# Reading the tile table two tiles ahead on TensorE, with the values kept in registers

## What is computed

```python
g = jnp.einsum('th,ehf->tef', x, w_gate)
u = jnp.einsum('th,ehf->tef', x, w_up)
act = jax.nn.silu(g) * u
act = act * combine[:, :, None]
moe_out = jnp.einsum('tef,efh->th', act, w_down)
```

## Time and profile before

| what | value |
|---|---|
| median of 3 runs | 1234.64 us (1233.26 to 1236.93) |
| the profiled execution | 1233.21 us, its span 1231.5 us |
| PE busy | 1161.2 us, 94% of the span |
| DVE, POOL, ACT busy | 729.4, 607.4, 512.1 us |
| mean granted TensorE clock | 0.994 of full speed |
| one product as the records show it | up (L1553) 399 ns, down (L1576) 390 ns, row turn (L1534) 276 ns |
| one result stored (L1035) | 256 KB, 2.1 us from issue to landing |

### The profile page before, as it was taken

The page is one execution under the profiler, slowest core; times in us unless marked ns, Lnnn a source line. Parts: engine busy times, 40 slices in busy tenths (PEclk is TensorE's granted clock), DMA queues, the critical chain, the costliest instruction groups (busy, mean ns, idle before and its releaser), DMA issues.

```text
span 1231.5 us, 21807 instructions
## 1 busy us (share of the span) xinstructions
PE 1161.2 (94%) x6020; PEld 776.9 (63%) x6021; DVE 729.4 (59%) x1083; ACT 512.1 (42%) x1056; POOL 607.4 (49%) x603
## 2 busy tenths in 40 slices
PE   1899999999999979999999999999999999999996
PEld 0334343433433346887888787877878777878885
DVE  5888888888888506773444433333333333338877
ACT  1577777777777731111111133333333333321110
POOL 3245645555454244056757345545644745228653
PEclk9999999999999999999999999999999999999998
DMA  9466676766675109944735155455454464433555
GB/s 236 127 189 184 194 192 187 186 189 193 180 193 164 58 35 361 379 161 132 266 127 188 53 161 205 153 189 185 165 193 154 162 209 157 145 94 106 161 170 188
DMA packets 104815, 214.58 MB, mean 174 GB/s; under 512 B 12352, under 2 KB 17472, under 8 KB 104768
## 3 DMA queue, kind: packets, MB, share of 16 engines
q1 hardware_dynamic: 85408, 152.08, 40.2%
q0 software_dynamic: 18016, 61.88, 15.4%
q10 hardware_dynamic: 1344, 0.04, 0.1%
HBM read 117.48 MB, written 91.75 MB: 170 GB/s over the span
## 4 chain that ended last, share of the span: by engine, by line
PE 61%; DVE 1%; issue 1%; DVEq 0%; ACT 0%
PE score_ps L135 19%; PE score_ps L1553 18%; PE d_ps L1508 9%; PE d_ps L1576 9%; PE score_ps L1534 3%; PE d_ps L1565 1%; PE d_ps L1461 1%; DVE y_all L1355 1%; DVE y_all L1343 0%; DVEq L158 0%; PE d_ps L1484 0%; PE score_ps L1470 0%; PE d_ps L1478 0%; DVE th L1420 0%; PE d_ps L1477 0%
## 5 line engine op out<-in xcount | busy, mean ns | idle before, releaser
L662 DVE TENSOR_REDUCE maxima<-score_ps 128x2 f32<-128x1024 f32 x256 | 301.5, 1218 | 49.8 <-PE score_ps L754 47.0
L609 ACT ACTIVATE probs<-sb_ps 128x512 f32<-128x512 f32 x512 | 262.8, 600 | 27.4 <-PE sb_ps L781 27.4
L135 PE MATMUL score_ps<-yn_t,w_split 128*128 128x512 f32 x1056 | 252.9, 398 | 3.1 <-POOL w_split L539 3.1
L1553 PE MATMUL score_ps<-w_split,x_split 128*128 x948 | 236.8, 399 | 0.0
L135 PEld LDWEIGHTS score_ps<-yn_t,w_split 128*128 128x128 f32 x1056 | 199.1, 189 | 51.6 <-POOL w_split L539 4.0
L1553 PEld LDWEIGHTS score_ps<-w_split,x_split 128*128 128x128 f32 x948 | 172.4, 188 | 33.1
L1072 POOL CAST w_split<-w_raw 128x1024 fp32r<-128x1024 f32 x63 | 65.9, 1046 | 241.8 <-POOLq L1142 141.4
L1074 POOL TENSOR_TENSOR w_split<-w_raw,w_split 128x1024 fp32r<-128x1024 f32 x63 | 151.9, 2410 | 5.2
L792 PE MATMUL o_ps<-probs,v_t 128*17 128x512 f32 x1024 | 135.6, 601 | 0.0
L1508 PE MATMUL d_ps<-w_split,h_split 128*128 128x512 f32 x528 | 124.4, 391 | 0.0
L1576 PE MATMUL d_ps<-w_split,h_rows 128*128 x474 | 120.4, 390 | 0.0
(11 more groups left out here) (149 smaller groups left out, 1324.3 us busy)
## 6 DMA issues: line engine op xcount, KB each, us to landing
xs_dram<-zero SPq DMA_DIRECT2D x1, 20224.0 KB, 58.7
stage<-xs_dram SPq DMA_DIRECT2D x79, 256.0 KB, 2.7
res_dram<-stage SPq DMA_DIRECT2D x79, 256.0 KB, 2.1
k_dram<-k_hi SPq DMA_DIRECT2D x16, 512.0 KB, 2.8
q_dram<-q_hi SPq DMA_DIRECT2D x16, 512.0 KB, 2.8
w_raw<-in_L_ffn_w_gate_dram POOLq DMA_DIRECT2D x16, 512.0 KB, 4.8
w_raw<-in_L_ffn_w_up_dram POOLq DMA_DIRECT2D x16, 512.0 KB, 6.1
w_raw<-in_L_ffn_w_down_dram POOLq DMA_DIRECT2D x16, 512.0 KB, 6.8
```

Source lines behind the costliest of these rows:

```text
L135: mm = pe.matmul(dst[i], w[:, k, f * P:(f + 1) * P], self.yn_t[:, b, k, t * self.SPAN:(t + 1) * self.SPAN], start=(n == 0), stop=(n == 3 * ...
L609: act.activation(probs[:, c % 2, head(j)[2], :], sb_ps[:, bank_of_score(HG * c + j), :], ACT.Exp, scale=SCALE).then_inc(exp_done, 1)
L662: dve.tensor_reduce(maxima[q % 2][:, :].rearrange("p (h u) -> p u h", u=8)[:, u, :], sa_ps[:, pair_of_unit(q, g, u), :, :], AX_X, ALU.max) ...
L1553: mm = pe.matmul(gu_ps[j], x_split[j][:, b, k, :], w_split[:, bass.ds(at + (a * 3 * ex.PIECE + k * 2 * FE), 2 * FE)], start=(n == 0), stop ...
```

## The change

PE reads both numbers of tile i + 2 between the up products of tile i + 1 and the down products of tile i. What was read is handed from tile to tile: `at` of the tile whose down products come next, and `need` and `at` of the tile after it. Over the loop's end three registers (`kept`) hold them. The third reading per tile (L1569) is gone, and none is left between the down products and the row turns.

```diff
+        def kept_values():
+
+            at, then = (pe.snap(kept[n], min_val=0, max_val=BUFFER) for n in (0, 2))
+            return at, (pe.snap(kept[1], min_val=3 * FIRST + 3, max_val=3 * (FIRST + NE)), then)
+
...
-        def down_rows(i, j):
-            at = pe.value_load(tables[0:1, bass.ds(i + P, 1)], min_val=0, max_val=BUFFER)
+        def down_rows(i, j, at):
...
-        def tile(i, j):
+        kept = [pe.alloc_register(f"kept{n}") for n in range(3)]
+        def tile(i, j, at, following):
             last = isinstance(i, int) and i == NTILE - 1
-            following = None if last else weights_of(i + 1)
             if ahead(i):
                 turn_rows(i + 2, j)
             turn_hidden(i, j)
-            if not last:
-                up(i + 1, 1 - j, following)
-                down_rows(i, j)
+            if last:
+                return None, None
+            up(i + 1, 1 - j, following)
+            second = weights_of(i + 2) if ahead(i) else None
+            down_rows(i, j, at)
+            return following[1], second
...
-        up(0, 0, weights_of(0))
+        at = weights_of(0)
+        following = weights_of(1)
+        up(0, 0, at)
+        at = at[1]
         for i in range(2):
-            tile(i, i)
+            at, following = tile(i, i, at, following)
+        for reg, value in zip(kept, (at, *following)):
+            pe.reg_mov(reg, value)
         with pe.Fori(1, (NTILE - 3) // 2) as r:
+            at, following = kept_values()
             for j in range(2):
                 pair[0] = r
-                tile(2 * r + j, j)
+                at, following = tile(2 * r + j, j, at, following)
+            for reg, value in zip(kept, (at, *following)):
+                pe.reg_mov(reg, value)
+        at, following = kept_values()
         for i in range(NTILE - 3, NTILE):
-            tile(i, i % 2)
+            last_at = at
+            at, following = tile(i, i % 2, at, following)
...
-        down_rows(NTILE - 1, (NTILE - 1) % 2)
+        down_rows(NTILE - 1, (NTILE - 1) % 2, last_at)
```

## The result

The changed kernel takes 1238.51 us (median of 8 runs, 1236.74 to 1241.13), the kernel before 1234.97 us (8 runs). The ratio is 1.0031, with a 95% interval of 1.0018 to 1.0044: 3.8 us slower by the ratio. It had 1236.5 us.

What follows compares the result with a forecast made beforehand. PE bounds the kernel, busy 94%, with its sequencer late at even tiles' row turns. Tiles 0, long loads +1.6, second meetings +0.8, less about 0.5, gave +1.9 on 1234.64: 1236.5 us, range 1229 to 1242.

Steps and rivals of the forecast that it cites:

- The loop's end: Late even-tile row turns cost 0.33 us per pair, 12.2 us in all; the hidden-values wait limits PE's gain to 5.2 us.
- The readings' new place: With a second 0.75 us reading between up and down products, the sequencer sets the even tile's down products' start, where it was.
- even tile 0: Term of the sum: the even tile's 0.14 us PE gain is waited away ahead of its down products, net 0.
- came out 0.02 early: Even tile's down products at 822.45 against 822.47 before; about 0.5 us was taken off the sum for it.
- The odd tile: Its two readings have room, since its load takes 302 ns and PE bounds what follows; counted as nothing.
- Slow loads: A reading that meets the store costs 0.27 us more; long even-tile loads over 580 ns add 1.57 us.
- the rival of 1246.5 us: Both readings of the even tile are slow, 0.27 us per pair, 10 us in all; chance 0.13.
- second meetings: Second readings that meet the late store's packets in perhaps one tile in twelve: 3 x 0.27 = 0.8 us.
- The readings fit: Rival: down products wait for PE again and the 5.2 us stay, 1229.4 us; chance 0.25.
- All of the 12.2 us: Rival: the hidden-values wait is earlier than thought, so all the loop's-end loss comes back, 1222.4 us; chance 0.03.
- nothing moves: Rival: the branch, not the even tile's first readings, held the row turns, 1234.6 us; chance 0.04.
- The sum: Even and odd tile 0, long loads +1.6, second meeting +0.8, less about 0.5: about +1.9 us.

Runs made afterwards that it cites:

- split kernel: Changed kernel, but only `at` is read between up and down products and `need` behind the down products: 1229.04 us, ratio 0.9953 to the kernel before.
- kernels with the waits first: Up products' waits for split weights and rows put ahead of the hidden-values wait: 1225.48 us with `need` read behind the down products, 1233.70 us in the changed kernel.
- kernels that split only one kind of tile: Changed kernel with `need` read behind the down products in even tiles only, 1228.88 us, or in odd tiles only, 1240.23 us.
- two kernels with a late store: SP issues the result's store only after the split of the next hidden values: 1248.31 us in the kernel before, 1237.95 us in the changed kernel.
- kernels with a third reading: Changed kernel plus one more, unused reading of `at` per tile between up and down products: 1264.44 us, ratio 1.0233 to the kernel before.
- both readings under the wait: Changed kernel with both readings moved behind the row turns, ahead of the wait for the hidden values: 1233.19 us, ratio 0.9981 to the kernel before.
- both readings behind the down products: Changed kernel with both readings moved from between up and down products to behind the down products: 1241.24 us, ratio 1.0048 to the kernel before.

## Why the prediction was right, and where it was off

**The loop's end.** Right. The 0.33 us ahead of the even tile's turns are gone, and not 12.2 us but about 5 are there to be won from it. The split kernel, where nothing else gets in the way, is 5.8 us faster by the ratio (1 - 0.9953), against 5.2 in the forecast. That the hidden values and the instructions behind their wait hold the up products is shown by the kernels with the waits first. The up products came 0.20 us earlier on the record, not 0.14, but as the forecast said this was waited away ahead of the down products.

**The readings' new place.** Right in mechanism, and mis-sized in one term. The forecast let the sequencer release the even tile's down products at the time of before, which makes a pair of 9.92 us plus the long loads. Measured over the loop it is 10.04, and the median of the single pairs has gone from 9.90 to 10.00. The term "even tile 0" is the one that was off: it measured 0.1 us per pair, 37 x 0.1 = 3.7 us. The forecast used rows rounded to 0.1 us, and it took every register instruction at its time of before. Read tile by tile, the eight up instructions of an even tile start within 0.93 us as a median and not 0.89, the second reading takes 0.78 and not 0.75, and the stretch from the second load's end to the first down instruction is 0.49 and not 0.45. From the first up to the first down instruction that makes 3.00 us where it was 2.15: 0.85 us were added, and the forecast had 0.75. There is no longer any slack in this chain to hide it. Why these instructions are slower is open. The 0.5 us taken off because the typical tile "came out 0.02 early" rested on a difference smaller than the rounding of its rows, and no run shows it.

**The odd tile** at nothing: right. The kernels that split only one kind of tile gave 6.2 us below the kernel before for the even tiles, and for the odd ones the changed kernel's time to within 0.2%.

**Slow loads.** The link with the store was an inference from coincidence, and the two kernels with a late store bear it out: the slow reading went with the store from one line to another. The second reading of the even tile stayed fast as forecast, 297 ns above, so the rival of 1246.5 us fell. The longest load of L1544 in the loop after its first rounds is 952 ns, and L1545's 832:

```profile
L1544 PEldq TENSOR_LOAD <-tables x72: 296/352/952, 716.9 to 1073.7; - x72
L1545 PEldq TENSOR_LOAD <-tables x72: 296/453/832, 717.6 to 1074.8; - x72
```

Their excess of 1.6 us and the 0.8 us for second meetings were about what was seen: over 37 even tiles the first loads exceed 580 ns by 2.0 us in all, one of 1114 ns at the loop's start included, and the second loads lie 0.9 us above their median, four of them at 448 to 580 ns. That the longest loads come "mostly while POOL's weight transfers run" is not enough as a cause: in the changed kernel with the late store those transfers run too, and none of its 148 loads takes over 319 ns. The store has to be there as well.

**The rivals.** "The readings fit" did not happen in the changed kernel, but its price was right: it is what the split kernel gives. "All of the 12.2 us" and "nothing moves" are excluded by PE's timeline. **The sum** said 1.9 us more than before; 3.5 by the medians and 3.8 by the ratio were measured. Direction and mechanism came out as forecast; that the loss stands at the 0.3% and not at half of it is the 0.1 us per pair that the term "even tile 0" lacked. The chance of "slower" was 0.24, and the interval of the ratio reaches to both sides of 0.3%.

## What to carry to other kernels

Where an engine's sequencer is only a little ahead of its engine, a register instruction or a scalar load costs nothing in one place and its full time in another. So before moving one, work out for each place how far ahead the sequencer is, from the last wait that stops it to the product that needs it. Moving two readings out of one gap and into another that had room for one gave a loss; leaving one in each place gave a gain of 0.5%. Taking waits that are already met from behind a late one gave another 0.05 us per pair there. And look at the first record of a group, not only at idle time: a stall of 0.1 us hides inside it.

## What the runs showed that I had not expected

A scalar load that meets the store's packets mostly takes 0.57 to 0.58 us instead of 0.30, and the effect follows the store when it is moved (L1570 at most 311 ns, L1540 579 ns). The fetch of rows does not do that. In the kernel before, a reading (L1539 at 822.1) took 303 ns with 287 GB/s of it moving, the last figure of this row:

```profile
822.12:822.42 0.30, 0.30 (x3) 0.26 (x2) 0.00 (x0) 0.00 (x0) 0.22 (x2) 1.00 0.75 287
```

The same register instructions took longer per group of eight in even tiles than in odd ones (from the first start to the last, medians of 0.93 and 0.88 us in the changed kernel; 0.92 to 0.93 against 0.87 to 0.91 in seven of its nine variants, and within 0.01 of one another in the kernels with a third reading and with both readings under the wait), with no wait among them.

Removing a covered reading and carrying its value in a register made the kernel 0.5% slower (both readings behind the down products), since writing the kept registers at the loop's end takes more of the sequencer than the branch alone: the record of L1627 there is 123 ns and that of L1621 140 ns, where L1605 had 32 and 68. That is 0.16 us more, and a pair took 0.15 us more.
